# VectorE's strips of a two-layer metaformer block: one loop over quads with the 16 strips written out

## What is computed

```python
# layer 0
x = x + L0_conv(_ln_c(x), qkv_w, qkv_b, proj_w, proj_b, rel_height, rel_width)
#   windows of 8x8 queries, 12x12 keys (2 of halo), 6 heads of 16; softmax; projection
t = _to_tokens(x); t = t + L0_ffn(_ln_t(t), W1, b1, W2, b2)   # 96 -> 384 -> relu -> 96
x = _from_tokens(t, x)
# layer 1
x = x + L1_conv(_ln_c(x), f_w, f_b, v_w, v_b, proj_w, proj_b, sim_alpha, sim_beta)
#   the picture folded 2x2 into quarters; 4 centres for each of 4 heads; sigmoid of the cosine,
#   each point kept at its best centre; gathered, spread back, projected
t = _to_tokens(x); t = t + L1_ffn(_ln_t(t), W1, b1, W2, b2)
x = _from_tokens(t, x)
```

## Time and profile before

| | us |
|---|---|
| median of 3 runs | 9184.56 |
| lowest, highest | 9182.27, 9190.45 |
| the profiled execution | 9189.38 |
| its span, first to last instruction | 9187.4 |
| TensorE busy | 7725.7 (84%) |
| VectorE busy | 7147.5 (78%) |
| ScalarE busy | 4849.8 (53%) |
| GpSimd busy | 2499.9 (27%) |

### The profile page before, as it was taken

One profiled execution on the slowest core, in us unless ns is written; L12 is line 12 of the kernel. 1 busy time (PEld: TensorE's weight loads), 2 busy tenths in 40 slices (PEclk: granted clock), 3 DMA queues, 4 the chain that ended last, 5 costly groups with the idle time before them and its releaser, 6 DMA issues.

```text
span 9187.4 us, 436110 instructions
## 1 busy us (share of the span) xinstructions
PE 7725.7 (84%) x172050; PEld 6181.7 (67%) x172050; DVE 7147.5 (78%) x23940; ACT 4849.8 (53%) x9750; POOL 2499.9 (27%) x4860
## 2 busy tenths in 40 slices
PE   6999999988888888888888888888888888887665
PEld 4777777776767666766766666766766666765443
DVE  3777777778888888887888878887888888887666
ACT  2555545545555555555555555555555555555445
POOL 1333332333223232232232222222232222232000
PEclk8999999999999999999999999998999999998556
DMA  2111111112222122222222222222222222221111
GB/s 59 47 43 44 51 47 48 50 52 52 61 56 60 55 54 59 55 56 56 58 54 59 55 54 58 56 56 55 60 54 59 55 54 59 55 57 51 58 57 59
DMA packets 193442, 502.56 MB, mean 55 GB/s; under 512 B 33508, under 2 KB 67108, under 8 KB 191468
## 3 DMA queue, kind: packets, MB, share of 16 engines
q1 hardware_dynamic: 191692, 476.75, 19.1%
HBM read 228.84 MB, written 169.93 MB: 43 GB/s over the span
## 4 chain that ended last, share of the span: by engine, by line
PE 52%; DVE 29%; issue 10%; ACT 6%; DVEq 1%; DMA 1%; SPq 0%; ACTq 0%; POOL 0%; POOLq 0%
PE scores_x L701 10%; PE flipped L723 6%; PE bank L605 4%; PE pv L751 3%; DVE maxes L1572 3%; PE bank L964 3%; PE bank L671 3%; PE misc L614 3%; DVE z L1687 2%; PE pv L745 2%; PE bank L991 2%; PE scores_x L641 2%; DVE shifted L1580 2%; PE bank L678 2%; DVE bn L1663 2%
## 5 line engine op out<-in xcount | busy, mean ns | idle before, releaser
L2022 POOL TENSOR_TENSOR vrest<-vstage,vmask 96x384 f32<-96x384 f32 x512 | 431.5, 843 | 4943.1 <-ACT vstage L1202 4943.0
L1572 DVE TENSOR_REDUCE maxes<-scores_x 128x6 f32<-128x864 f32 x1024 | 1078.9, 1054 | 727.0 <-PE scores_x L701 643.2
L701 PE MATMUL scores_x<-keys,queries 64*64 64x144 f32 x24576 | 1084.5, 310 | 552.6 <-DVE shifted L1580 541.2
L701 PEld LDWEIGHTS scores_x<-keys,queries 64*64 64x64 f32 x24576 | 788.6, 142 | 767.2 <-issue 715.5
L1239 ACT ACTIVATE probs<-flipped 128x384 f32<-128x384 f32 x1024 | 500.3, 489 | 1216.9 <-PE flipped L723 1214.7
L1580 DVE TENSOR_TENSOR shifted<-scores_x,maxes 128x768 f32<-128x768 f32 x1024 | 970.7, 948 | 0.8
L660 PE MATMUL bank<-xt,wq 97*32 97x64 f32 x24576 | 868.8, 223 | 93.9 <-issue 59.7
L663 PE MATMUL bank<-xn,wq 97*32 97x64 f32 x24576 | 889.4, 223 | 53.5 <-issue 53.1
L660 PEld LDWEIGHTS bank<-xt,wq 97*32 97x32 f32 x24576 | 740.8, 111 | 282.1 <-issue 195.2
L1190 ACT ACTIVATE queries<-bank 128x512 f32<-128x512 f32 x768 | 459.6, 598 | 881.3 <-PE bank L663 881.3
L723 PE MATMUL flipped<-ident,shifted 128*128 128x128 f32 x6144 | 902.4, 286 | 0.0
(11 more groups left out here) (189 smaller groups left out, 17432.4 us busy)
## 6 DMA issues: line engine op xcount, KB each, us to landing
keys<-kst SPq DMA_DIRECT2D x768, 99.0 KB
x_in<-x_dram SPq DMA_DIRECT2D x130, 396.0 KB
xn_kept<-xn SPq DMA_DIRECT2D x128, 388.0 KB, 3.8
later<-xn_kept SPq DMA_DIRECT2D x128, 388.0 KB, 3.4
x_tok<-tok_dram SPq DMA_DIRECT2D x128, 384.0 KB, 3.4
x_kept<-x SPq DMA_DIRECT2D x128, 384.0 KB, 2.3
later<-x_kept SPq DMA_DIRECT2D x128, 384.0 KB, 3.7
out_dram<-later SPq DMA_DIRECT2D x128, 384.0 KB, 2.4
```

The costliest lines, as they stand in the source:

```text
L701: last = mm(score[e][64 * j:64 * j + 64, g * NKEY:(g + 1) * NKEY], queries[64 * e:64 * e + 64, g, w, :], keys[64 * e:64 * e + 64, g, :, WS ...
L1572: V.tensor_reduce(maxes[:, p % 2, :, :], sc, AX.X, ALU.max).then_inc(max_ready.sem, 1)
```

## The change

VectorE's program alone is written differently. Every strip of quads 0, 1, 2 and 7 is now straight code with its number as a constant. The outer loop over quads 3 to 6 stays, and its body has the edge and the 16 strips in a row, their number being r x 16 + 2 + k with r in a register. The drains keep their loops. The work, the semaphores and their values are the same, and so is the other engines' order. VectorE's built program has 16,761 instructions where it had 4,083; the body of the loop over quads has 4,715.

```diff
-            with dve.Fori(0, STRIPS) as s:
-                strip(s + 2, stage(2), s)
+            for k in range(STRIPS):
+                strip(k + 2, stage(2), k)
             edge(1, LAG_B, True, False)
-            with dve.Fori(0, STRIPS) as s:
-                strip(s + LAG_B, stage(LAG_B), s)
+            for k in range(STRIPS):
+                strip(k + LAG_B, stage(LAG_B), k)
             edge(2, LAG_C, True, True)
-            strip(LAG_C, stage(LAG_C), 0, 0)
-            strip(LAG_C + 1, stage(LAG_C + 1), 1, 1)
-            with dve.Fori(0, STRIPS // 2 - 1) as s:
-                for par in range(2):
-                    strip(2 * s + (LAG_C + 2 + par), stage(LAG_C + 2), 2 * s + (2 + par), par)
+            for k in range(STRIPS):
+                strip(LAG_C + k, stage(LAG_C + k), k, k % 2)
             with dve.Fori(3, 7) as r:
                 edge(r, r * STRIPS + 2, True, True)
-                with dve.Fori(0, STRIPS // 2) as s:
-                    for par in range(2):
-                        strip(r * STRIPS + 2 * s + (2 + par), stage(LAG_C + 2), 2 * s + par, par)
+                for k in range(STRIPS):
+                    strip(r * STRIPS + (2 + k), stage(LAG_C + 2), k, k % 2)
             edge(7, 7 * STRIPS + 2, True, True)
-            with dve.Fori(0, STRIPS // 2 - 2) as s:
-                for par in range(2):
-                    strip(2 * s + (7 * STRIPS + 2 + par), stage(LAG_C + 2), 2 * s + par, par)
-            strip(N - 2, stage(N - 2), STRIPS - 4, 0)
-            strip(N - 1, stage(N - 1), STRIPS - 3, 1)
+            for k in range(STRIPS - 2):
+                strip(7 * STRIPS + 2 + k, stage(7 * STRIPS + 2 + k), k, k % 2)
```

## The result

| | before | after |
|---|---|---|
| median, us | 9183.42 | 9053.2 |
| lowest, highest (4 runs each) | 9181.35, 9190.45 | 9050.6, 9056.02 |
| the profiled execution | 9189.38 | 9054.27 |
| its span | 9187.4 | 9052.3 |

The account below looks back on a forecast made before the run. VectorE's idle at backward branches of the pair loop, 39 turns of 2.13 us, was taken to hold up TensorE; 86 us for turns plus 8 for constants, 94 off 9184.6, gave 9090 us, 8-in-10 range 9050 to 9112.

Parts of the forecast that it names:

- a change of the clock in quads 0 and 1: Quads 0 and 1: strips could switch between 52.97 and 50.28 us kinds; 43 us less, or 16 us more.
- register operations that might all be on the path: Mid-strip register operations, counted as nothing; were all on the path, 40 us more gain over 58 strips.
- Parts 1 and 2: Pair loops of quads 2 to 7: 39 turns go, 86 us less; three outer turns at quads 4 to 6 stay, 6.3 us.
- not below 5: Sign of being right: TensorE's longest wait at shifted falls from over 7 us to under 5 us.
- Part 5: Quads 3 to 6: with the gap gone, each strip has TensorE's 4.72 us wait; no new wait takes its place.
- Part 1's sum: Pair-loop turns, quads 2 to 7: 83.2 us idle plus 3.1 us of earlier starts, taken as 86 us; other end 80.7.
- the rival on the fetch: Quads 0 and 1: straight code waits for up to 119 more packets, 253 us slower, 9343 us; chance 0.04.
- Part 3: Quads 0 and 1: their loops turned without idle time, so writing them out removes no gap and adds code to fetch.
- Part 4: Quads 0, 1, 2, 7: strip numbers become constants; 42 strips at simw times 0.2, 8 us less; simw waits 122 to 80.
- The upper end of 48: Upper bound for registers becoming constants: 8 us at simw plus 40 us if all mid-strip register operations were on the path.
- The rule against it: The skill's 108 ns per compare-and-branch would make the 39 turns worth 4 us, time 9172; the trace's 2.13 us was believed.
- More than the sum: Rival: half of the 32 strips in quads 0 and 1 become faster by 2.7 us, 43 us more gain, 9047; chance 0.08.

Follow-up runs that it names:

- moved by 43: The kernel before with 43 semaphore increments more in the set-up of VectorE's program, no strip instruction changed: 9157.55 us, ratio 0.9979.
- quads 0 and 1 alone: The kernel before with only VectorE's one-strip loops of quads 0 and 1 written out: 9177.66 us, ratio 1.0011 to its own runs of before.
- the run with four strips a turn: The kernel before with four strips instead of two to a turn of VectorE's inner loop in quads 3 to 6: 9126.29 us, ratio 0.9945.
- the one other place that was tried: The changed kernel with 64 semaphore increments more in the set-up of VectorE's program: 9053.67 us, ratio 0.9866.
- the shift by 101 alone: The kernel before with 101 semaphore increments more in the set-up of VectorE's program, nothing else: 9170.06 us, ratio 0.999.

## Why the prediction was right, and where it was small

The measured time lies inside the range by 3 us at its lower end, and 36 of the 130 us were in no term of the sum. The range had been drawn that low for two reasons, a change of the clock in quads 0 and 1 and register operations that might all be on the path. The first did not come and of the second some 12 us came. So the turns, two thirds of the gain, were understood, and that the range still held the time was in part luck.

**Parts 1 and 2** held. The 39 waits went, three stayed at pooled, and the prices were 83.2 and 5.7 us where 83.2 and 6.3 had been read. Parity went (66.5 and 66.9 us), and TensorE's longest wait for shifted fell from 8.1 to 5.9 us, not below 5. **Part 5** held too: nothing took the gap's place, and TensorE's wait fell by what was removed.

**Part 1's sum** missed what a loop costs besides its turns. Its own words in the rival on the fetch show the failing step: "the next issue idle of the engine is 6.5 us in 32 pieces of at most 0.2 us" was used as a bound on the harm that straight code could do. It was a harm already being done, at one fixed step of every pair, with a second one (+0.37 us at L1805) that no issue row shows, since there the wait was put down to TensorE. Together 18.3 us of tail seams, of which 14.6 went.

**Part 3** was wrong in "removes no gap" as the whole of it: quad 1 gained 12 us. And it left out that writing quads 0 and 1 out moves the loops behind them, which by the account is worth from -21 us (moved by 43) to +25 us (quads 0 and 1 alone) in this kernel, up to twice its gain.

**Part 4** named the right operation and the right count: simw's waits fell from 122 to 80. The size per strip is 0.18 us. Quad 1 in before and after:

```profile
1484.27 0.29 DVE L1788 TENSOR_TENSOR winners<-ranks,best 128x128 f32<-128x128 f32 x1
1484.78 0.29 DVE L1793 TENSOR_TENSOR simw<-winners,sims 128x128 f32<-128x128 f32 x1 [0.22 <-DVE winners L1788]
```

```profile
1471.89 0.29 DVE L1788 TENSOR_TENSOR winners<-ranks,best 128x128 f32<-128x128 f32 x1
1472.22 0.29 DVE L1793 TENSOR_TENSOR simw<-winners,sims 128x128 f32<-128x128 f32 x1
```

For quads 2 and 7 the 5 us follow. For quad 1, 16 x 0.18 = 3 us of the 12 are explained. There the gap from a reduction to shifted_r also fell, from 0.12 to 0.035 us seven times a strip, 0.6 us a strip or 10 in the quad. In quads 2 and 7 the same gaps fell and the next reduction's wait for TensorE took it all back, as the text assumed; in quad 1 not all of it seems to have been taken back. The upper end of 48 covered that, the taken value did not.

**The rule against it.** The Trainium skill (Advanced Engine Details and Errata, Control Flow Timing) has about 108 ns for a compare-and-branch. Single turns stood for 0.4 to 3.4 us in the kernels here, most for about 2, and removing them gave what the rows said. The Trainium skill also says (Runtime: NRT & Kernel Launch, Instruction fetch mechanics) that fetching straight code over a block's end is mostly hidden. In the strip's head it costs nothing, by TensorE's pace; in the tail, where nothing takes a stop up, the traces show 0.12 to 0.37 us at a seam.

**The rival of the fetch** expected up to 119 packets more. Written out alone, quads 0 and 1 brought 29 (378 against 349) and no idle time of a turn's size. In the changed kernel the packets fell to 271 all the same, since the turns that went had brought more: 3.25 each in the run with four strips a turn.

"More than the sum" put its surplus in quad 0's two kinds of strips, where nothing came. Its time (9047) was closer than the forecast, and its reason was not the one found.

## What to carry to other kernels

The loop body of 591 instructions here cost its turns (about 2 us each; the bodies of 180 and 227 showed none) and, beside them, stops at fixed steps of the body, paid at every turn. Before believing a small change in such a kernel, move the loops by some idle instructions: 43 of them were worth 19 us here, as much as an edit with reasons. Straight code of four times the size showed no cost of its own, and at the one other place that was tried its time was the same within the intervals. A row of short waits with a count equal to a loop's turns deserves to be multiplied out, not used as a ceiling.

## What was not expected of the hardware

- VectorE stops at places 128 instructions apart, or a multiple, for 0.12 to 0.37 us. A stop costs time where the next instruction waits for nothing but VectorE's own last result (L1668) or where the wait for TensorE is already over (L1805), and not where the next wait for TensorE takes it up.
- The backward branch over the same pair body in quads 3 to 6 took 2.0 to 3.05 us on average, with the place of the loop in the program (single turns 1.5 to 3.4), and this changed by 1 us within two instructions.
- A register operation between two dependent VectorE instructions costs 0.09 us (0.123 to 0.034 us from the reduction to shifted_r); what stands at simw costs 0.18.
- With four strips a turn, 3.25 packets of 8.2 KB less were carried for each turn left out. The count depends on the place as well: the shift by 101 alone took 32 packets away.
